# Attention's end, its turn, linear layer and next layernorm in one stage by node tile; 80 edge tiles placed by GpSimd scatters; edge attributes turned in pairs

## The reference, cut to what matters

```
# third layer, graph attention: its end
out = agg.reshape(N, H * C) / (denom + 1e-16)     # in the kernel the division stands here
out = (out + bias) @ lin_w + lin_b
x   = x + maximum(out, 0)
xn  = _layernorm(x)                               # input of the fourth layer
# fifth layer, message passing
edge_in = concatenate([h[row], h[col], edge_attr])      # 256 + 256 + 64
msg = relu(edge_in @ W1.T + b1) @ W2.T + b2
agg = segment_sum(msg, row)
```

## Time and profile before

| | us |
|---|---|
| median of 3 runs | 5867.91 (5867.34 to 5868.26) |
| the profiled execution's own time | 5852.53 |
| its span | 5850.8 |
| placing stage, first to last DVE instruction | 93.25 to 330.69 |
| attention's end with the layernorm | 3019.66 to 3099.11 |
| edge update, first to last | 3672.05 to 4331 (about) |
| PE, DVE, ACT, POOL busy over the span | 82%, 54%, 23%, 54% |

### The profile page before, as it was taken

One profiled execution on the slowest core, in us unless ns is written; L12 is line 12 of the kernel. 1 busy time (PEld: TensorE's weight loads), 2 busy tenths in 40 slices (PEclk: granted clock), 3 DMA queues, 4 the chain that ended last, 5 costly groups with the idle time before them and its releaser, 6 DMA issues. The chain is left out here.

```text
span 5850.8 us, 74399 instructions
## 1 busy us (share of the span) xinstructions
PE 4793.1 (82%) x20458; PEld 2904.0 (50%) x20459; DVE 3170.6 (54%) x7606; ACT 1333.6 (23%) x3259; POOL 3178.7 (54%) x3560
## 2 busy tenths in 40 slices
PE   7968887788768599979985998999997678888674
PEld 2223434433345411118864997788874433333364
DVE  8964444444355577768984114566667433444432
ACT  4940002000032222222213333333332121000121
POOL 3237774777615577746633776667630212777324
PEclk7979999999978755559997999999998789999887
DMA  5013332333411267765525765333330533333265
GB/s 214 11 56 105 103 104 66 106 105 105 95 29 37 78 204 216 216 198 149 159 79 187 219 219 153 112 115 114 114 73 1 154 118 125 105 105 104 50 195 170
DMA packets 392381, 711.85 MB, mean 122 GB/s; under 512 B 117999, under 2 KB 257327, under 8 KB 391663
## 3 DMA queue, kind: packets, MB, share of 16 engines
q0 software_dynamic: 131680, 340.14, 21.3%
q1 hardware_dynamic: 257152, 364.49, 19.5%
q10 hardware_dynamic: 3216, 3.28, 0.2%
HBM read 532.97 MB, written 174.69 MB: 121 GB/s over the span
## 5 line engine op out<-in xcount | busy, mean ns | idle before, releaser
L795 PE MATMUL ps<-wide 128*128 128x256 f32 x2640 | 915.2, 429 | 309.8 <-DMA wide<-table,src 179.8
L822 DVE TENSOR_TENSOR wide<-wide,ps 128x256 f32 x1320 | 555.0, 420 | 968.2 <-PE ps L795 965.2
L780 POOL DMA_INDIRECT wide<-table,src x880 | 846.0, 961 | 276.5 <-PE ps L795 205.0
L795 PEld LDWEIGHTS ps<-wide 128*128 128x128 f32 x2640 | 405.4, 189 | 834.4 <-DMA wide<-table,src 547.4
L792 PE MATMUL ps<-zerow,zerob 128*128 128x440 bf16 x2640 | 712.1, 352 | 27.8 <-DVE wide L127 27.8
L780 POOL DMA_INDIRECT wide<-table_rel,rel x440 | 423.4, 962 | 332.4 <-ACTq L96 198.7
L2777 POOL DMA_INDIRECT work<-table,work x440 | 448.3, 1019 | 190.9 <-issue 106.7
L1669 POOL DMA_INDIRECT wide<-table_gat,src x440 | 427.0, 970 | 135.3 <-issue 133.9
L792 PEld LDWEIGHTS ps<-zerow,zerob 128*128 128x128 bf16 x2640 | 259.2, 98 | 221.9 <-DVE wide L127 29.5
L1838 POOL TENSOR_TENSOR wide<-wide,work 128x1024 f32<-128x1024 f32 x110 | 222.2, 2020 | 197.3 <-ACT work L1822 197.3
L1763 DVE TENSOR_REDUCE work<-ps 128x8 f32<-128x1024 f32 x220 | 269.0, 1223 | 103.9 <-PE ps L1729 100.2
(11 more groups left out here) (522 smaller groups left out, 8647.0 us busy)
## 6 DMA issues: line engine op xcount, KB each, us to landing
edge_rows<-wide SPq DMA_DIRECT2D x110, 532.0 KB, 3.2
wide<-edge_rows SPq DMA_DIRECT2D x110, 532.0 KB
normed<-in_L_ffn_W SPq DMA_DIRECT2D x42, 1024.0 KB
table_rel<-wide SPq DMA_DIRECT2D x25, 1024.0 KB, 4.4
wide<-in_L_ffn_expert_w SPq DMA_DIRECT2D x90, 256.0 KB, 3.1
work<-rec SPq DMA_DIRECT2D x110, 136.0 KB, 2.1
rec<-work SPq DMA_DIRECT2D x27, 544.0 KB, 16.3
normed_T<-in_L_ffn_W SPq DMA_DIRECT2D x14, 1024.0 KB
```

The lines of the kernel that those rows point to most:

```text
L780: nc.gpsimd.indirect_dma_start(rows[:, w % RT, :], None, table, bass.IndirectOffsetOnAxis(ap=index[:, w:w + 1], axis=0)).then_inc(gathered ...
L795: nc.tensor.matmul(m.PS[:, w % (2 * Q), 0:D], S[:, w % RT, :], rows[:, w % RT, :], start=True, stop=True).then_inc(summed, 1)
L822: v.tensor_tensor(at, at, m.PS[:, s, 0:D], ALU.add).then_inc(added, 1)
```

## The change

Three parts, in three places.

1. **Placing.** The first `STRAIGHT = 80` input tiles no longer go through ACT, DVE and PE. DVE computes each edge's address (`row_e * 441 + col_e`) and puts its two numbers side by side; POOL writes these pairs of 8 bytes by 80 indirect DMAs to an array `placed` in memory, ahead of its record groups. `placed` is zeroed by one more SP transfer in `sort_slots`. SP reads it back (128 rows of 3.5 KB) when it has come to the fifth record group, and DVE adds it in two more instructions at the end.
2. **Attention's end.** The four stages become one, `attention_end`. POOL divides tile by tile. The bias before the linear layer goes through the weights once (transpose, copy, multiply) and is added with the other bias. PE alternates, for each step n, the transposes of tile n, the product of tile n - 1, and the transposes of the normalised tile n - 8; ACT evicts tile n, normalises tile n - 7, evicts tile n - 8; DVE adds, takes the maximum, adds to the residual and takes the statistics.
3. **Edge update.** Attributes come by a transfer of their own (512 runs of 256 bytes a quad), the two index words by another (512 runs of 8 bytes), both from `rec2`. Two edge tiles' attributes (2 x 64 columns) are transposed at once, so two float32 transposes a quad and not four. Their product uses a block-diagonal weight of 128 x 512, first in the bank, and the `by_src` products are added. `wa` is blanked in full by POOL, and SP waits for that before its first load.

```diff
+STRAIGHT = 80
@@ sort_slots, sync
+                sp.dma_start(m.placed.rearrange("(p w) c -> p (w c)", p=P), m.zeros[:, 0:2 * WP]
+                             ).then_inc(m.placed_blanked, 16)
@@ place_edges
-            for t in range(ET):
+            for t in range(STRAIGHT, ET):            # ACT, DVE and PE alike
...
         def _(pool):
+            pool.wait_ge(m.placed_blanked, 16)
+            pool.wait_ge(paired, 3)
+            for t in range(STRAIGHT):
+                nc.gpsimd.indirect_dma_start(m.placed, bass.IndirectOffsetOnAxis(ap=where_i[:, t:t + 1], axis=0),
+                                             pairs[:, t, :], None).then_inc(scattered, 16)
...
             for g in range(PLACED):
+                if g == RING:
+                    sp.wait_ge(scattered, 16 * STRAIGHT)
+                    sp.dma_start(back, m.placed.rearrange("(p w) c -> p w c", p=P)).then_inc(returned, 16)
@@ attention_end (new; the four stages before go)
+        def _(pool):
+            pool.wait_ge(ready, 1)
+            for t in range(NT):
+                nc.gpsimd.tensor_tensor(to, of, rd[:, t, :].unsqueeze(2).to_broadcast([P, H, C]), ALU.mult
+                                        ).then_inc(scaled, 1)
+        def _(pe):
+            pe.wait_ge(loaded, 48)
...
+            for n in range(NT + LAG + 1):                       # LAG = 7
+                if n < NT:
+                    pe.wait_ge(scaled, n + 1)
...
+                if 1 <= n <= NT:
+                    multiply(n - 1)
+                t = n - LAG - 1
+                if t >= 0:
+                    pe.wait_ge(normed, t + 1)
...
+        def _(act):
+            for n in range(NT + LAG + 1):
...
+                if n % U == 0 and 0 < n <= NT:
+                    g = n // U - 1
+                    act.wait_ge(vared, g + 1)
+                    nc.scalar.activation(rstd[:, mine], rstd[:, mine], ACT.Sqrt).then_inc(rooted, 1)
@@ edge_update
-                sp.dma_start(rec[:, u * Q:(u + 1) * Q, :], r[:, bass.ds(j * Q, Q), :]).then_inc(came[u], 16)
+                sp.dma_start(ends[:, u * Q:(u + 1) * Q, :], r[:, bass.ds(j * Q, Q), EA:EA + 2]).then_inc(came[u], 16)
+                sp.dma_start(attrs[:, u * Q * EA:(u + 1) * Q * EA].rearrange("p (s c) -> p s c", s=Q),
+                             r[:, bass.ds(j * Q, Q), 0:EA]).then_inc(came[u], 16)
...
-                    mm = te.transpose(m.PS[0:EA, 1, s * P:(s + 1) * P], rec[:, u * Q + s, 0:EA], m.ident[:])
+                for k in range(PAIRS):
+                    mm = te.transpose(m.PS[:, 1, k * P:(k + 1) * P], attrs[:, at:at + P], m.ident[:])
...
-                    te.matmul(at, ST[:, k, :], tile_at(by_src, tiles[s]), start=True, stop=False)
-                    mm = te.matmul(at, attT[:, k, :], wa, start=False, stop=True)
+                    te.matmul(m.PS[:, 2 + k, :], attT[:, u % RS * PAIRS + k, :], wa, start=True, stop=False)
+                    for s in range(2 * k, 2 * k + 2):
+                        mm = te.matmul(at, ST[:, u % RS * Q + s, :], tile_at(by_src, tiles[s]), start=False,
+                                       stop=(s % 2 == 1))
```

More of the change, by code:

```diff
@@ L458, in place_edges @@
         below = [view(m.BB, o + 5 * WT + ET + k * WP, WP) for k in range(2)]
+        o += 5 * WT + ET + 2 * WP
+        upper = [view(m.BB, o + k * WT, WT) for k in range(2)]
+        back = view(m.BB, o + 2 * WT, WP, 2)
+        pairs = view(m.BB, o + 2 * WT + 2 * WP, STRAIGHT, 2)
+        where = view(m.BB, o + 2 * WT + 2 * WP + 2 * STRAIGHT, STRAIGHT)
+        where_i = view(m.BB, o + 2 * WT + 2 * WP + 3 * STRAIGHT, STRAIGHT).bitcast(I32)
+        first = slice(0, STRAIGHT)
         block = st.block()
@@ L491, in _ @@
             c.step(v.tensor_scalar(near, m.oth_d, float(HALF), None, ALU.subtract))
-            for t in range(ET):
+            c.step(v.scalar_tensor_tensor(where, m.row_e[:, first], float(WP), m.col_e[:, first], ALU.mult, ALU.add))
+            v.tensor_copy(where_i, where).then_inc(paired, 1)
+            v.tensor_copy(pairs[:, :, 0], both[:, first]).then_inc(paired, 1)
+            v.tensor_copy(pairs[:, :, 1], near[:, first]).then_inc(paired, 1)
+            for t in range(STRAIGHT, ET):
                 u, at = t % R, slice(t, t + 1)
-                if t >= R:
-                    dve.wait_ge(used, t - R + 1)
+                if t >= STRAIGHT + R:
+                    dve.wait_ge(used, t - STRAIGHT - R + 1)
                 v.tensor_scalar(cols[0][:, u, :], m.iotah[:, 0:P], m.row_e[:, at], both[:, at], ALU.is_equal,
@@ L521, in _ @@
                           skip_group_check=True)
-            for t in range(ET):
-                pe.wait_ge(hot, t + 1)
-                pe.wait_ge(stepped, t + 1)
+            for t in range(STRAIGHT, ET):
+                pe.wait_ge(hot, t - STRAIGHT + 1)
+                pe.wait_ge(stepped, t - STRAIGHT + 1)
                 for k in range(2):
@@ L1953, in _, with finish, shifts @@
             c.step(v.tensor_scalar(rd, m.AGG[:, :, D:RW], 1e-16, None, ALU.add))
[L1954 to L1966, removed]
+            v.reciprocal(rd, rd).then_inc(ready, 1)
+            dve.wait_ge(loaded, 48)
+            dve.wait_ge(based, 1)
+            c.step(v.tensor_tensor(base, m.PS[:, 7, 0:D], b, ALU.add))
+            def finish(t):
+                dve.wait_ge(made, t + 1)
+                v.tensor_tensor(total[:, t % 2, :], m.PS[:, 2 + t % 2, 0:D], base, ALU.add).then_inc(summed, 1)
+                dve.wait_ge(summed, t + 1)
+                at = m.X[:, t, :]
+                v.scalar_tensor_tensor(at, total[:, t % 2, :], 0.0, at, ALU.max, ALU.add).then_inc(added, 1)
+                dve.wait_ge(added, t + 1)
+                return v.bn_stats(stats[:, t, :], at)
+            def shifts(g):
+                mine = slice(g * U, g * U + U)
+                dve.wait_ge(rooted, g + 1)
+                c.step(v.reciprocal(rstd[:, mine], rstd[:, mine]))
+                v.scalar_tensor_tensor(shift[:, mine], mv[:, mine, 0], -1.0, rstd[:, mine], ALU.mult, ALU.mult
+                                       ).then_inc(shifted, 1)
+            for t in range(NT):
+                ins = finish(t)
+                if t % U == 0 and t:
+                    shifts(t // U - 1)
+                if t % U == U - 1:
+                    g = t // U
+                    mine = slice(g * U, g * U + U)
+                    c.step(ins)
+                    for s in range(g * U, g * U + U):
+                        ins = v.bn_aggr(mv[:, s, :], stats[:, s, :])
+                    c.step(ins)
+                    v.tensor_scalar(rstd[:, mine], mv[:, mine, 1], EPS, None, ALU.add).then_inc(vared, 1)
+            shifts(GROUPS - 1)
 def expert_of(nc, eng, m, w, ne):
```

132 lines of the change are left out of this document (101 added, 31 removed).

## The result

| | before | after |
|---|---|---|
| median, us | 5868.09 (5867.34 to 5874.42, 4 runs) | 5804.8 (5798.15 to 5812.34, 4 runs) |
| ratio | 1 | 0.989 (0.9879 to 0.9902) |
| profiled execution, its own time | 5852.53 | 5812.34 |
| its span | 5850.8 | 5810.6 |

The kernel became 63.3 us (1.1%) faster. All twelve experiments ran later, on four chips on which the kernel before takes 6561 to 6630 us. On the one of them where the changed kernel ran as it is, it is slower than the kernel before: 1.0068 (1.0055 to 1.0082). Both results are real, and most of the experiments are about the slowdown. I call the four the second to the fifth chip. The number of the chip of the first measurement is not on record, and nothing separates a difference between chips from one between sessions; where I write "on the first chip", both are meant.

What follows compares the result with a forecast made beforehand. ACT was taken to bound placing, four stages without overlap attention's end, and PE the edge update. Gains 33.5 + 24 + 22 = 79.5 us; 79 off the 5867.9 median gave 5789 us, range 5772 to 5820.

Steps and rivals of the forecast that it cites:

- The bound changes from ACT to POOL in the placing: Placing: with 80 tiles moved to scatters, POOL ends the stage at 298.2 against 289 for the others; gain 33.5 us.
- SP then waits for the last landing, some 2.2 us: Placing's end: after POOL ends near 295, SP's 2.2 us wait; next stage starts 1.05 us later, at 298.2.
- Attention's end: Four stages of 79.5 us become one of 55.3 us, bound by DVE at 1.47 us a tile; gain 24 us.
- the lower bound of the part: Attention's end: every group stalled by 1.5 us and DVE held up by POOL while it divides; gain 14 us.
- the lock of the Trainium skill: Placing: rule that DVE locks GpSimd out of their shared port, making scatters slower than 1.27 us; covered by upper bound.
- Edge update: Two float32 transposes fewer save 0.22 us a quad, 24 us over 110; start costs 2 us; net gain 22 us.
- Unchanged stages cost nothing: Stages outside the three parts: taken as the same, so 79 us came straight off the median.
- A: Placing: POOL's scatters do not bound it (pitch under 1.15), the others end it; 9 us more gained, 5780; chance 0.12.
- B: Merged attention stage locks step: each tile costs the sum, 2.1 us; 16 us more, 5805; chance 0.15.
- C: Edge update: 8-byte runs clog DMA engines; over 140 ns each eats all gains, 200 ns gives 6120; chance 0.06.
- D: Edge update: PE gains nothing because weight loads set the transposes' pace; 22 us less gain, 5811; chance 0.15.

## Why the prediction was right, and where it wasn't

The forecast was 5789, the result 5804.8: right in sign and inside the range, 15.8 us off. That it is no further off is in part luck. The steps below lose 5.9 + 4.4 + 1.7 us in the three stages and 12.7 in unchanged code, 24.7 in all, and the profiled execution, which the sum put at 5773, took 5812. By its steps:

- **The bound changes from ACT to POOL in the placing**: right on the first chip. ACT's last start 279.3 for 279.0, DVE's end 288.2 for 288, scatters from 96.9 at 1.27 us, last record done at 297.3 for 295.
- **"SP then waits for the last landing, some 2.2 us"**: the step that failed there. SP was released 1.3 us after the last transfer, but POOL's own drain ended 6.0 us after it. Gain 27.6 and not 33.5. The prediction took the landing (2.2 us) as the last wait and gave the drain nothing. The drain of before was in its trace, with the same 5.9 us; I had read only instructions that count as busy.
- **Attention's end**: 59.9 for 55.3. The group of five tiles took 7.65 us for the 7.75 of the sum (five at 1.47 and 0.4), and the tail from the last statistics (3051.46) 7.0 for 7.35. The miss is the one instruction of 4.94 us; with it paced the stage came to 55.3. I had weighed POOL's division by its own length (0.61 for 0.6); what its row does to DVE stood only in the lower bound of the part. A smaller reading was wrong without effect: PE's product of a tile takes 1.03 us warm and not 0.86, which was DVE's pace, and PE still did not bound. I had read the lock of the Trainium skill (SBUF - State Buffer, SBUF: two separate sides) as speaking for part 1. The page also says that, for a DVE operation with two SBUF inputs, it holds only against a GpSimd operation that reads SBUF, and that the later one waits. That is the case of attention's end. What the trace adds is that DVE waited not for one division of 0.61 us but for the whole unbroken row.
- **Edge update**: 5.63 us a quad to the digit, DMA share 0.49 for 0.48. The start cost 3.9 us and not 2 (first L2991 17.9 us into the stage, before 14.0). Gain 20.3 for 22.
- **Unchanged stages cost nothing** ("the stages are the same"): wrong by 7.0 us in this execution, since POOL's memset slid onto DVE's instruction, and by 5.7, since the router stage met the half clock.
- **Rivals on the first chip**: A, no: the pitch is 1.27. B, no: 1.53 us a tile and not 2.1. C, no: 0.49 (its threshold is off besides: 512 runs that add 0.74 us to a quad of 5.63 are runs of 128 ns, not 140). D, no: the quad is shorter by the 0.22 us of two transposes.
- **The other side**: with the placing in it, the change is slower on four chips, by a mechanism that none of my rivals had. I took POOL's indirect transfers as free for the others because the earlier trace rows show ACT full beside them. That row holds for one chip. For the chip of the prediction it was right.

## What to carry to other kernels

When a list gets short enough that POOL sets the end of a stage, add the drain of its sequencer to the sum. It was 6 us here behind the last indirect transfer and 3.3 to 13.7 in other stages, so read it in the stage itself, where it is still hidden. Before work goes from PE to POOL's indirect transfers, see whether the others keep their pace beside them on more than one chip: here the same edit gave 27.6 us in its stage on one and made the kernel 62 and 74 us slower on two others. Work that no edit touches can still change its time, by what it now runs beside and by the clock that it now meets: 12.7 us here. A helper engine that runs ahead without need can hold up the one it helps; pacing it by a wait gave 4.6 us back.

## What the runs showed of the hardware

- On the four chips of the experiments PE, ACT and DVE got through a tile, two matmuls of 441 columns, in 5.6 us while POOL issued indirect transfers, 2.8 us a matmul, and in the usual 0.55 as soon as POOL stopped. In the first measurement there was no such effect. Of the 860 us between the changed kernel's two profiles (first and second chip), 167 lie in the placing, 87, 82 and 85 in three aggregations, 104 in the first half of the attention and 84 in the edge update, all with such transfers. It is no rule for every such stage: one with 60 of them (183.5 and 183.3 us) was no longer.
- PE's busy time doesn't show it (3.10 us for eight matmuls that took 22.4). What shows it is an engine that waits for "remote" on a ring whose tiles PE's records call done.
- In the placing stage POOL's drain ended 5.9 to 6.0 us after its last indirect transfer in twelve of the fourteen traces, whether that was at 194, 294, 297 or 307 us, and 6.3 and 8.2 in the two others. In other stages it ended 3.3 to 13.7 us after it.
- A DVE instruction with two SBUF inputs waited 4.5 us for an unbroken row of POOL's products (it took 4.94 to 5.52 us in seven traces, 0.62 in the two with POOL paced). One with a single SBUF input took 6.32 us beside a memset of POOL, though by its record it began 0.56 us before it.
- 8-byte scatters took as long as those of 272 bytes: 0.96 us, 1.27 us apart.
